# LSTM and graph convolution merged into one program, with two normalized groups made inside the LSTM

## The reference, cut to what matters

```python
for p in range(1, MAX_SKIP + 1):           # 1..4
    nw = Tv // p
    wins = h[:, :nw * p, :].reshape(Bv * nw, p, Hd)
    last = _lstm_last(Wih[p - 1], Whh[p - 1], bih[p - 1], bhh[p - 1], wins)
    h = h.at[:, idx, :].set(last.reshape(Bv, nw, Hd))
x = _layernorm(x + h)                       # first norm
...
A_norm = A + jnp.eye(n)                     # layer 1
deg = jnp.sum(A_norm, axis=0) + jnp.sum(A_norm, axis=1) - jnp.diagonal(A_norm)
A_hat = A_norm * rsqrt(deg)[:, None] * rsqrt(deg)[None, :]
agg = jnp.einsum('nm,bmd->bnd', A_hat, features)
h = relu(_batchnorm(agg.reshape(-1, d) @ W1.T + b1, g1, be1))
```

## Time and profile before

| | |
|---|---|
| time of three runs, median (lowest to highest) | 2104.67 us (2098.53 to 2105.48) |
| the profiled execution: time, span | 2098.44 us, 2096.3 us |
| granted TensorE clock, mean | 0.963 of full speed |
| PE busy, matmuls | 1946.0 us (93%), x11833 |
| DVE busy | 1490.4 us (71%) |
| ACT busy | 1143.2 us (55%) |
| POOL busy | 753.5 us (36%) |

### The profile page before, as it was taken

How to read it: one execution, slowest core, us unless ns; L and a number is a source line. 1 busy time by engine, 2 the same in 40 slices (tenths; PEclk the granted TensorE clock), 3 DMA queues, 4 the chain that set the end, 5 groups by cost and what they waited for, 6 DMA issues and landing times. The chain is left out here.

```text
span 2096.3 us, 32718 instructions
## 1 busy us (share of the span) xinstructions
PE 1946.0 (93%) x11833; PEld 1650.6 (79%) x11833; DVE 1490.4 (71%) x3823; ACT 1143.2 (55%) x1803; POOL 753.5 (36%) x1924
## 2 busy tenths in 40 slices
PE   6999898999999999999999959989889899699996
PEld 6999776788889999988888758866689634469896
DVE  5676666666656676788888858968566479788675
ACT  2444565545444454444444247747667589566675
POOL 2333345543444554000000046656544000106775
PEclk8999899999999999999999969999989999899998
DMA  3110101000000000000000043203222000003122
GB/s 113 41 42 1 41 1 40 1 1 20 21 1 1 1 1 1 1 1 0 1 1 1 1 126 112 91 21 99 72 71 71 21 1 1 11 21 115 40 71 81
DMA packets 65631, 71.15 MB, mean 34 GB/s; under 512 B 3767, under 2 KB 63294, under 8 KB 65470
## 3 DMA queue, kind: packets, MB, share of 16 engines
q1 hardware_dynamic: 65470, 69.07, 10.3%
HBM read 43.90 MB, written 25.17 MB: 33 GB/s over the span
## 5 line engine op out<-in xcount | busy, mean ns | idle before, releaser
L1749 ACT ACTIVATE l_gates<-l_acc,l_b 128x512 f32<-128x512 f32 (+1 forms) x504 | 300.1, 633 | 95.3 <-PE l_acc L473 93.0
L1756 ACT ACTIVATE l_gates<-l_cell 128x512 f32<-128x512 f32 (+1 forms) x144 | 83.9, 583 | 252.1 <-DVE l_cell L1808 151.5
L471 PE MATMUL l_acc<-l_x_hi,l_w1x_hi 128*128 128x336 f32 (+1 forms) x544 | 191.5, 352 | 19.4 <-DVE l_x_lo L1719 10.6
L472 PE MATMUL l_acc<-l_x_hi,l_w1x_lo 128*128 128x336 f32 (+1 forms) x544 | 191.3, 352 | 0.0
L473 PE MATMUL l_acc<-l_x_lo,l_w1x_hi 128*128 128x336 f32 (+1 forms) x544 | 191.1, 351 | 0.0
L1709 ACT ACTIVATE l_x_hi<-hT 128x512 fp32r<-128x512 f32 (+1 forms) x144 | 101.0, 755 | 162.6 <-PE l_acc L473 162.6
L471 PE MATMUL l_acc<-l_x_hi,l_w0x_hi 128*128 128x512 f32 x464 | 181.0, 390 | 3.0 <-DVE l_x_lo L1719 2.5
L472 PE MATMUL l_acc<-l_x_hi,l_w0x_lo 128*128 128x512 f32 x464 | 180.6, 389 | 0.0
L473 PE MATMUL l_acc<-l_x_lo,l_w0x_hi 128*128 128x512 f32 x464 | 180.5, 389 | 0.0
L183 POOL TENSOR_SCALAR bi_shifted<-bi_shifted 32x1 f32<-32x1 f32 x62 | 35.6, 574 | 400.5 <-DVE bi_shifted L173 400.5
L660 POOL MEMSET n_power<- 128x4 f32 x1 | 0.1, 106 | 385.5 <-POOLq L2276 385.5
(11 more groups left out here) (513 smaller groups left out, 6224.6 us busy)
## 6 DMA issues: line engine op xcount, KB each, us to landing
xin<-in_x SPq DMA_DIRECT2D x16, 512.0 KB, 3.8
hidB<-in_x SPq DMA_DIRECT2D x16, 512.0 KB, 4.8
x<-hT SPq DMA_DIRECT2D x16, 512.0 KB, 3.2
hidB<-x SPq DMA_DIRECT2D x16, 512.0 KB, 3.9
x<-hidB SPq DMA_DIRECT2D x16, 512.0 KB, 2.9
attention_residual<-x SPq DMA_DIRECT2D x16, 512.0 KB, 3.9
out_x<-hT SPq DMA_DIRECT2D x16, 512.0 KB, 2.9
l_rawx<-in_wih SPq DMA_DIRECT2D x4, 1024.0 KB, 4.9
```

The lines of the kernel that those rows point to most:

```text
L471: t.matmul(out, left[0], right[0], start=start, stop=False)
L472: t.matmul(out, left[1], right[0], start=False, stop=False)
L1749: i = a.activation(gates[:, j, q, 0:n], acc[:, j, q, 0:n], FUNC[q], bias=b[:, o:o + 1])
L1756: a.activation(tcell[:, j, 0:n], cell[:, j, 0:n], TANH).then_inc(tc, 1)
```

## The change

Five things are changed.
1. `first_layers` builds the LSTM and the convolution into one block: each engine's convolution stream follows its LSTM stream without a barrier. The buffers of both are laid out so that the early ones don't overlap. `convolution_and_projections` now returns functions, and three more (`beside_scalar`, `beside_vector`, `beside_tensor`) that the LSTM calls inside its p = 4 groups.
2. In groups 1 to 3 of p = 4, after the input products of k = 0, TensorE writes into the forget gate's two banks (`spare`): in group 1 the row sums for the matrix, in groups 2 and 3 the transposes of rows groups 0 and 1. The forget gate's input products of k = 1 are moved behind those of the other gates, and wait until VectorE has read the banks.
3. VectorE, GpSimd and ScalarE make the two groups' sums, statistics, parameters and scaling, the matrix, the split of w1 and y of group 0 at fixed places of p = 4. Group 2's and group 3's transposes are moved behind the first mixing product and the first projection.
4. SyncE loads w1, the batch norm's parameters and x of groups 0 to 2 when p = 4 begins; x of group 3, w2 and the edge indices after the first mixing output.
5. The table of reflections has one more line: for p = 2 and k = 0, but for group 0, a reflection in the second unit.

```diff
             elif p == 1 and group % 2 == 0:
                 here = [(u, u + 1, update_last)]
+            elif p == 2 and k == 0 and group:
+                here = [(u + 1, u + 1, update_last)]
             elif p in (2, 3) and k:
...
+                    late = p == SKIP and k == 1
                     for j in range(2):
...
                         for q in used(k):
+                            if late and q == FORGET:
+                                continue
+                            i = input_products(j, q)
                             if k == 0 and (j, q) != LAST:
                                 i.then_inc(gate_mm, 1)
+                    if late:
+                        ahead(pe, group, False)
+                        for j in range(2):
+                            i = input_products(j, FORGET)
                     i.then_inc(x_used, 1)
+                    if p == SKIP and k == 0:
+                        ahead(pe, group, True)
...
+        def beside_tensor(pe, group, begin):
+            if begin and group == 1:
+                pe.wait_ge(scaled, 1)
+                nc.tensor.matmul(spare[:, 0, 0:P], c["ones"][:, :], tmp, start=True, stop=True).then_inc(rowed, 1)
+            elif begin and group >= 2:
+                pe.wait_ge(lstm["hidden"], lstm["last"] * 2 + lstm["group_units"])
+                for r in range(TILES):
+                    for ch in range(C):
+                        i = nc.tensor.transpose(spare_tr[:, r // 2, r % 2, ch * P:(ch + 1) * P],
+                                                group_of(hT, group - 2)[:, ch, r * P:(r + 1) * P], c["ident"][:, :])
+                i.then_inc(tr, 1)
+            elif group == 1:
+                pe.wait_ge(mat_done, 1)
+            elif group >= 2:
+                pe.wait_ge(n1.summed, group - 1)
...
+            if group >= 2 and (k, j) == (0, 0):
+                dve.wait_ge(tr, group - 1)
+                dve.wait_ge(res_in[group - 2], 16)
+                v.tensor_tensor(halves[0][:, 0], spare_tr[:, 0], halves[1][:, 0], ALU.add)
+                n1.sum(v, spare_tr[:, 1], halves[1][:, 1], halves[0][:, 1])
+            if group >= 2 and (k, j) == (0, 1):
+                n1.statistics(v, dve, rows(hT, group - 2), group - 2)
...
+        def beside_scalar(act, group, k, j):
+            if k and j:
+                if (group, k) == (1, 1):
+                    act.wait_ge(w_in, 16)
+                    nc.scalar.activation(wa[0][:, :], raw_w1, ACT.Copy).then_inc(w_hi, 1)
+                if (group, k) == (2, 1):
+                    act.wait_ge(mat_done, 1)
+                    nc.scalar.activation(A[0][:, :], a1, ACT.Copy).then_inc(mat_hi, 1)
+                    n1.scale(nc.scalar, act, rows(hT, 0), 0)
+                if (group, k) == (2, 2):
+                    y_hi(act, 0)
+                if (group, k) == (3, 1):
+                    n1.scale(nc.scalar, act, rows(hT, 1), 1)
...
+            pool.wait_ge(lstm["hidden"], DONE)
+            pool.wait_ge(mix, 1)
+            set_constants()
+            n1.params(p, pool, 2)
+            y_lo(1)
...
+            pe.wait_ge(mat_lo, 1)
+            pe.wait_ge(READ, DONE - 1)
+            for g in range(GROUPS):
...
+                if g == 0:
+                    transposes(2)
+                    pe.wait_ge(w_lo, 1)
+                    pe.wait_ge(READ, DONE)
+                elif g + 3 < GROUPS:
+                    transposes(g + 3)
...
+                if g == 0:
+                    transposes(3)
```

More of the change, by code:

```diff
@@ L549, in convolution_and_projections @@
         stats1, stats2 = sb("bn1_stats", [P, HC, GROUPS, 6]), sb("bn2_stats", [P, C, GROUPS, 6])
[L550 to L565, removed]
+        count, by_node, prod, runs = sb("e_count", [P, E]), sb("e_by_node", [P, E]), sb("e_prod", [N, E]), sb("e_runs", [P, E])
         ps_tr = ctx.enter_context(nc.psum_tensor("c_tr", [P, TILES, D], F32))
@@ new lines, in on_gpsimd @@
+            pool.wait_ge(mix, GROUPS * C)
+            pool.wait_ge(ranked, 1)
+            s = Seq(pool, e_pool)
+            for k in range(EC):
+                s.after(p.tensor_scalar(perm[:, k, :], count[:, :], rank[:, k:k + 1], None, ALU.is_equal))
+                for n in range(2):
+                    s.after(p.tensor_scalar(hot[:, k, n, :], count[:, 0:N], col[:, n, k:k + 1], None, ALU.is_equal))
+            hot_src, hot_dst = (hot[:, :, n, :].bitcast(F32) for n in range(2))
+            s.after(p.tensor_tensor(both[:, :, 0, :], hot_src, hot_dst, ALU.add))
@@ new lines, in on_gpsimd, with y_hi @@
+            pool.wait_ge(bno, GROUPS + 1)
+            batch_norm(par2, n2.power[:, 0:C], bn2_ready)
+            for g in range(GROUPS):
+                n2.params(p, pool, g)
+        def y_hi(act, g):
+            act.wait_ge(n1.out, g + 1)
+            if g >= 2:
+                act.wait_ge(mix, (g - 1) * C)
+            elif g:
+                act.wait_ge(lstm["hidden"], DONE)
+            nc.scalar.activation(ys[g % 2][0][:, :, :], rows(hT, g), ACT.Copy).then_inc(yh, 1)
+        def beside_scalar(act, group, k, j):
[11 more added lines that the diff above has]
+                    n1.scale(nc.scalar, act, rows(hT, 1), 1)
@@ L927, in edge_masks @@
-                def edge_masks(e):
-                    for n in ("start", "last"):
-                        e.after(v.tensor_scalar(m["keep_" + n][:, :], m["drop_" + n][:, :], -1.0, 1.0, ALU.mult, ALU.add))
-                        e.after(v.tensor_scalar(m["drop_" + n][:, :], m["drop_" + n][:, :], -BIG, None, ALU.mult))
-                def output_stats(g):
-                    dve.wait_ge(out, g + 1)
-                    for k in range(C):
-                        i = v.bn_stats(stats2[:, k, g, :], group_of(hT, g)[:, k])
-                    i.then_inc(bno, 1)
@@ L1859, in _ @@
             graph[3](dve, lambda s: rows_low(dve, s))
-            lstm[3](dve)
+            lstm[3](dve, ahead[1])
+            conv[3](dve)
         @block.tensor
@@ L1864, in _ @@
             graph[4](pe)
-            lstm[4](pe)
+            lstm[4](pe, ahead[2])
+            conv[4](pe)
+    return m, spectral, scores, place, hidB
 class RowNorm:
@@ L1883, in add, with sum, statistics @@
     def add(self, v, dve, psum, res, rows, g):
+        self.sum(v, psum, res, rows)
+        self.statistics(v, dve, rows, g)
+    def sum(self, v, psum, res, rows):
         v.tensor_tensor(rows, psum, res, ALU.add).then_inc(self.summed, 1)
+    def statistics(self, v, dve, rows, g):
         dve.wait_ge(self.summed, g + 1)
```

1004 lines of the change are left out of this document (520 added, 484 removed).

## The result

The changed kernel takes 2147.39 us (median of four runs, 2145.22 to 2148.1) against 2103.39 before (2098.53 to 2105.48): a ratio of 1.0211, 95% interval 1.0191 to 1.0231. It is slower by 44.0 us.

A forecast was written before the change was run, and what follows sets the result against it. TensorE was taken to set the LSTM's pace, with the reflection chain over VectorE and GpSimd stretching windows of two; -24.0 + 0 + 51 = +27 on 2098.44 gives 2125.5, raised for run spread to 2129 us, range 2100 to 2150.

The forecast's parts named there:

- the likeliest case: The forecast's own case, LSTM stretched and boundary shortened as computed: 2112 to 2145 us, chance 0.62.
- Part 3, the third reflection: In windows of two, one more reflection in seven groups makes a group 36.7 us against TensorE's 29.9: +51 us.
- the three turns: Successive VectorE and GpSimd turns in a group of p = 2: 14.4, 8.3 and 14.0 us, 36.7 in all.
- the two bounds: GpSimd's part beside VectorE in p = 2: always 5.1 us gives +25; 7.8 and 8.8 us give +67.
- The boundary: Between LSTM and convolution, the first mixing product follows directly and group 1's projection comes earlier: 24.0 us gained.
- two pauses of about 3 us: At the boundary, TensorE pauses twice before group 1's projection; 1.0 us was added for the lowered clock.
- the lag isn't carried on: In windows of three, reflections stand as before, so the delay from windows of two adds nothing more.
- Part 2: Work put into windows of four: VectorE's share is hidden and the net cost is 0; 5 us if not hidden.
- The two terms: In windows of four, 2.0 us for TensorE's 17 added products against 2.0 saved from the last group's search stalls.
- The sum: Whole run: -24.0 + 0 + 51 = +27 us.
- The first: Rival: windows of two aren't stretched, leaving the boundary's -24 alone, 2074 to 2081 us; chance 0.12.
- The fourth: Rival: GpSimd stands still whenever VectorE runs 512-column products; 39.2 us a group in p = 2, +69, 2147 us; chance 0.05.

The follow-up runs named there:

- e3: The changed kernel with update and next front of the three reflections in p = 2 ahead of the unit's own work: 2118.48 us, ratio 1.008.
- e1: The changed kernel without the new line in the table of reflections, all else of the change kept: 2091.36 us, ratio 0.9945.
- e11: The same kernel as e1, run once more on another chip: 2090.16 us, ratio 0.9952.
- e4: The changed kernel with 12 instead of 19 search steps in each group of p = 3, the rest moved to p = 4: 2140.19 us, ratio 1.0179.
- e9: e1's kernel with one of the search's six rounds left out and 34 instead of 40 steps in each group of p = 4: 2081.3 us, ratio 0.9909.
- e6: e1's kernel with three instead of two search steps ahead of the second unit in p = 4: 2098.68 us, ratio 0.9982.
- e2: The kernel before with only the new line of the table of reflections added: 2153.56 us, ratio 1.0248.
- e5: e1's kernel with GpSimd's two large subtractions beside the LSTM waiting until VectorE has made that step's h_lo: 2091.63 us, ratio 0.9953.
- e8: The changed kernel without its new table line, with the edits of e5, e6 and e7 together: 2096.38 us, ratio 0.9975.
- e7: e1's kernel with GpSimd's y_lo of group 1 ahead of group 2's parameters instead of behind them: 2096.05 us, ratio 0.9971.
- e10: e1's kernel with nine instead of seven search steps ahead of the first unit in p = 3: 2095.11 us, ratio 0.9967.

## Why the prediction came out as it did

**The direction and the main cause were right.** A time of 2147 stands inside 2100 to 2150, above the likeliest case's own 2112 to 2145, and 18 us above the 2129 named.

**Part 3, the third reflection: right in its mechanism and its turns; that the total is met within 1 us is in part luck.** +51 was predicted. The first recurrent product of three rows starts at 693.08, before at 643.01: +50.1. One group of the changed kernel, GpSimd's L183 (start) and L244 (end) for the three turns:

```profile
477.80 0.23 POOL L183 TENSOR_SCALAR bi_shifted<-bi_shifted 32x1 f32<-32x1 f32 x1 [7.65 <-DVE bi_shifted L173]
482.58 0.30 POOL L244 TENSOR_TENSOR bi_shifted<-bi_shifted 32x58 f32<-32x58 f32 x1
486.06 1.21 POOL L183 TENSOR_SCALAR bi_shifted<-bi_shifted 32x1 f32<-32x1 f32 x1 [3.18 <-DVE bi_shifted L173]
493.33 0.30 POOL L244 TENSOR_TENSOR bi_shifted<-bi_shifted 32x56 f32<-32x56 f32 x1
500.18 0.60 POOL L183 TENSOR_SCALAR bi_shifted<-bi_shifted 32x1 f32<-32x1 f32 x1 [6.55 <-DVE bi_shifted L173]
506.38 0.29 POOL L244 TENSOR_TENSOR bi_shifted<-bi_shifted 32x54 f32<-32x54 f32 x1
```

GpSimd's part took 5.1 (beside nothing), 7.6 (beside a unit and the splitting) and 6.5 us (beside one unit), for 5.1, 7.5 and 6.7 predicted; the turns between fronts 8.25, 14.1 and 14.1 for 8.3, 14.0 and 14.4. Group 1 takes 34.4 us and the others 35.5 to 36.6, for 36.7, and group 4, at the half, 41.0, where two weight differences of 2.27 us lie beside an L183 of 5.01. The choice between the two bounds fell right, and e3 shows that it is this chain: shorter turns with the same work give 26 us back in these windows.

The end of the chain shows the luck, on VectorE and TensorE of the changed kernel:

```profile
683.55 0.65 PE L471 MATMUL l_acc<-l_x_hi,l_w1x_hi 128*128 128x336 f32 x1 [4.70 <-ACT l_gates L1854]
689.27 0.53 DVE L1929 TENSOR_TENSOR l_h_lo<-l_gates,l_h_hi 128x336 fp32r<-128x336 f32 x1
692.92 0.31 PE L473 MATMUL l_acc<-l_x_lo,l_w1x_hi 128*128 128x336 f32 x1
693.08 0.32 PE L471 MATMUL l_acc<-l_h_hi,l_w1h_hi 128*128 128x336 f32 x1
```

The sum had this h_lo at 694.2; it is done at 689.80, 4.4 us sooner, since the chain began 1.5 us earlier than in the sum and its seven groups took 257.9 us for 260.7. TensorE started the recurrent product 3.3 us behind it and without a wait, because the pause of 4.70 us had put off its input products: a term that the sum didn't have. The sum also counted from TensorE's start before, 643.01, and not from the h_lo of then, done at 640.19. From h_lo to h_lo it says +54, and the traces +49.6.

**The boundary: right.** Predicted were 24.0 us, group 1's projection 21.3 us behind the last product; it is 20.8 behind (1299.03 less 1278.2), and the boundary gives 24.4 there and 22.9 from group 2 on. The 1.5 us between the two are the clock. From group 1's projection to group 2's, before, in the changed kernel, in e1 and in e11, in this order:

```profile
1258.31:1267.51 9.20, 9.20 (x60) 7.96 (x58) 8.54 (x15) 6.62 (x12) 5.35 (x15) 1.00 0.38 116
```

```profile
1299.03:1309.75 10.72, 10.72 (x58) 9.25 (x57) 8.04 (x14) 6.15 (x11) 6.80 (x15) 0.84 0.32 98
```

```profile
1245.59:1254.72 9.13, 9.13 (x56) 8.03 (x57) 8.33 (x15) 6.38 (x12) 6.94 (x15) 1.00 0.37 117
```

```profile
1244.17:1254.94 10.77, 10.77 (x56) 9.26 (x57) 8.41 (x15) 7.00 (x12) 9.61 (x18) 0.83 0.31 99
```

At a granted clock of 1.00 the stretch takes 9.1 to 9.2 us, at 0.84 and 0.83 it takes 10.7 to 10.8, and e1 and e11 are the same kernel. So a difference of 1.6 us at group 2's projection says nothing of an edit. Of the two pauses of about 3 us that were foreseen, only the second came (3.22 us); the first was 0.45.

**The step that failed is the sentence behind the sum of part 3**: "In windows of three the reflections stand as before, and the lag isn't carried on." They don't. By the two kernels' tables p = 3 has 10 reflections and 83 steps of the search where it had 17 and 34: the search begins in group 3 and no longer in group 6. Part 2 did count on a search that ends early, but not on where its steps go. In p = 3 VectorE's work changed from the first of these rows (before) to the second (after):

```profile
645.00:917.60 272.60, 270.42 (x1746) 269.49 (x1745) 193.84 (x659) 134.02 (x262) 100.58 (x242) 0.99 0.00 1
```

```profile
695.00:976.80 281.80, 273.88 (x1745) 271.87 (x1744) 215.13 (x716) 133.54 (x262) 53.43 (x136) 0.98 0.00 1
```

21.3 us more on VectorE, at 76% busy, cost 9.0 us. VectorE is not full over the stretch, but at single places: seven steps of the search, 5.0 us, lie ahead of a cell whose result TensorE wants, and where the end and start of a round, or the weights' split, come on top, TensorE stops:

```profile
829.59 0.65 PE L471 MATMUL l_acc<-l_x_hi,l_w1x_hi 128*128 128x336 f32 x1 [3.81 <-ACT l_gates L1854]
964.17 0.42 PE L471 MATMUL l_acc<-l_h_hi,l_w1h_hi 128*128 128x336 f32 x1 [1.80 <-DVE l_h_lo L1929]
```

TensorE's waits of over 0.4 us in p = 3 add up to 7.9 us, before to 2.2. e4 took steps out of p = 3 and got 6.7 us back there. The lag wasn't inherited, it was made anew, by work that the prediction had not followed to its new place.

**Part 2, predicted 0, was +6.0.** The two terms weighed against each other were the wrong ones. TensorE's 2.0 us for the 17 products fits what e9 leaves. What was called hidden, "behind them in its queue stands the second half of the same step", is VectorE's work, and VectorE has little room in p = 4: e6 added 2.2 us a group and lost 1.4 to 3.2 by it, e1 shows 11.3 us more VectorE work and 8.7 us more time, e9 the reverse. The changed kernel pays only 6.0 because the new line has emptied its last group of the search (74.3 us there); 78.8 and 76.4 are the groups before it. The fair comparison is e2, which has the same line and none of the work beside the LSTM: from the first hT of p = 3's group 7 to the last hT it takes 300.2 us and the changed kernel 309.0, so the work costs 8.8 us here too. Most of that has a place. GpSimd's large subtraction meets h_lo:

```profile
1088.93 2.44 POOL L727 TENSOR_TENSOR wa_lo<-hidB,wa_hi 128x1024 fp32r<-128x1024 f32 x1 [80.75 <-ACT wa_hi L800]
1089.19 2.72 DVE L1929 TENSOR_TENSOR l_h_lo<-l_gates,l_h_hi 128x512 fp32r<-128x512 f32 x1
1091.97 0.79 PE L471 MATMUL l_acc<-l_h_hi,l_w0h_hi 128*128 128x512 f32 x1 [3.50 <-DVE l_h_lo L1929]
```

TensorE waits 3.50 us for that h_lo, in e2 0.46 at the same place, and behind the wait its granted clock is 0.50 for 5.5 us; in the next 5.5 it makes 25 products instead of 13:

```profile
1091.97:1097.50 5.53, 5.53 (x13) 4.37 (x14) 5.00 (x24) 0.70 (x2) 0.00 (x0) 0.50 0.01 3
1097.50:1103.00 5.50, 5.50 (x25) 4.49 (x25) 3.70 (x11) 3.17 (x5) 0.00 (x0) 0.98 0.00 0
```

That is 3.0 us of wait and some 2.6 of clock; with 2.0 for the 17 products 7.6 of the 8.8 are found. The other large subtraction holds an h_lo too (2.77 us at 1189.34), and TensorE doesn't wait behind it. e5 took both out of e1's kernel and gained nothing, since other waits grew there. Whether it would gain here, where one of them stops TensorE for longer, wasn't tried.

**The sum as it came out**: 50.1 + 9.0 + 6.0 - 22.9 = +42.2, for +27 predicted. The medians differ by 44.0.

**The rivals.** The first, that the LSTM isn't stretched, would have been the case of e1, and even there the time is 2091 and not 2074 to 2081. The fourth named the measured 2147, but not for its reason: a group took 36.4 us and not the 39.2 of a full exclusion.

What stays open: how much of p = 4's loss in the changed kernel belongs to each piece of the work beside it. VectorE's total was varied, and the two large subtractions were moved, both in e1's kernel alone. Also not tried is a matrix or a norm left where it was.

## What to carry to other kernels

Two engines that hand small work to and fro form a chain whose length is the sum of its turns. An engine's idle time is no cover for one turn more; add the turns up, and compare them with what the pacing engine needs. Where turns must be added, let the other engine's part begin ahead of the long work and not behind it (26 us here).

When a table moves work up, follow everything that comes after it in the same table. Here the background search slid into stretches that were full at single places, and cost 9 us that no edited line shows; at the end it gave 2.8 back (e2).

Called hidden because its result is wanted late, 11 us of work on an engine at 84% of a stretch cost 9, the 2 us of TensorE's own products included. Before calling such work hidden, try what an extra microsecond on that engine costs. And count a wait of TensorE with the slower products behind it: one of 3.5 us cost some 2.6 us more in clock.

## What the runs showed of the hardware beyond that

A GpSimd subtraction of 128x1024 with two SBUF inputs (2.4 to 2.5 us) held back the VectorE instruction with two SBUF inputs that met it until it ended: 2.72 to 2.78 us for an h_lo of 0.69, 2.03 for an L110 of 0.13. A VectorE subtraction of the same size with one input in PSUM went through beside it (VectorE and GpSimd of the changed kernel):

```profile
1296.29 2.37 POOL L725 TENSOR_TENSOR y<-hT,y 128x1024 fp32r<-128x1024 f32 x1
1296.73 0.69 DVE L962 TENSOR_TENSOR ax<-c_mix,ax 128x512 fp32r<-128x512 f32 x1 [4.57 <-ACT ax L825]
```

In the chain of small operations the hindrance is mild, and on GpSimd's side alone: it takes 6.5 and 7.6 us for 5.1, and the VectorE instructions of 128x512 beside it keep their 0.67 to 0.69. Only beside the two weight differences does a small GpSimd instruction stand for long (5.01 us for an L183). The sentence of the Trainium skill cited in the prediction (Advanced Engine Details and Errata, VectorE Performance Modes) speaks of GpSimd and two-port VectorE instructions. The same section gives tensor_tensor, the kind of h_lo, no two-port mode, so the sentence doesn't cover the blocking of h_lo that the traces show.

The stretch behind the boundary has a length of its own. From group 2's projection to the end of the span the thirteen profiled executions, with the same instructions there, take 828.2 to 836.2 us: 828 to 829 in three (before, e2, e6) and 833 to 836 in the ten others. Its last part in e6 and in e8:

```profile
1900.00:2089.00 189.00, 170.25 (x1768) 157.33 (x1767) 132.61 (x201) 128.05 (x194) 134.65 (x396) 0.97 0.24 76
```

```profile
1900.00:2097.00 197.00, 178.52 (x1852) 165.14 (x1850) 135.92 (x205) 131.43 (x199) 137.64 (x407) 0.93 0.23 76
```

TensorE's granted clock is 0.97 in the one and 0.93 in the other. e6 and e8 reach group 2's projection at 1261.23 and 1261.25 us and end 8 us apart. That is as much as e6, e7, e8 and e10 differ from e1 (4.7 to 7.3 us). What is said of them therefore rests on the places in the trace ahead of that stretch. That the same kernel takes either length is likely (e6's ten executions ran from 2091.33 to 2100.43) but not shown, since no kernel has a trace of both lengths. What decides which of the clocks an execution gets stays open.
